# Two causal self attentions of a decoder's first layer: queries and keys stored as three bf16 parts, repeated by the loads

## The reference

```python
scores = (einsum('bhnd,bhmd->bhnm', q_r, k_r) + einsum('bhnd,bhmd->bhnm', q_i, k_i)) / sqrt(hd)
probs = softmax(where(causal, scores, -inf))          # 4 x 16 heads of 256 x 256
...
att = einsum('bhqd,bhkd->bhqk', q, k) * scale          # second attention, d = 8
y = einsum('bhqk,bhkd->bhqd', softmax(where(causal, att, -inf)), v)
```

## Time and profile before

| | before |
|---|---|
| median of three runs | 2439.69 us |
| the three runs | 2427.64, 2544.63, 2439.69 us |
| the profiled execution | 2427.71 us, of which 2425.9 us from the first to the last instruction |
| TensorE's mean granted clock | 0.854 of 2.4 GHz |
| busy shares | PE 78%, DVE 51%, ACT 39%, POOL 21% |
| `p0`: first store to first load of `a0` | 28.18 to 62.99 us |
| `a0`: first load to the end of the block | 62.99 to about 160 us |
| `p1`: first store to first store of `c0` | 189.00 to 223.65 us |
| `a1`: first load to the first load of `ac` | 313.19 to 408.17 us |

### The profile page before, as it was taken

How to read it: one execution, slowest core, us unless ns; L and a number is a source line. 1 busy time by engine, 2 the same in 40 slices (tenths; PEclk the granted TensorE clock), 3 DMA queues, 4 the chain that set the end, 5 groups by cost and what they waited for, 6 DMA issues and landing times. The chain is left out here.

```text
span 2425.9 us, 44544 instructions
## 1 busy us (share of the span) xinstructions
PE 1897.7 (78%) x16613; PEld 1031.0 (42%) x16613; DVE 1242.4 (51%) x2710; ACT 946.8 (39%) x1346; POOL 512.7 (21%) x360
## 2 busy tenths in 40 slices
PE   2764366888889826998899588439999999997497
PEld 1542243233233423664455356314444444554365
DVE  2663267888788233335843356344555555551322
ACT  1432143266566422221155135222555555453133
POOL 2112112000000000002644100002545444543100
PEclk7885578699799857998999789765999999998699
DMA  8416922132222021100000000011222112210010
GB/s 230 106 41 199 292 56 67 47 82 68 68 62 62 15 92 39 39 26 0 1 1 2 1 1 15 11 44 29 47 49 46 35 42 49 47 24 1 18 35 26
DMA packets 171185, 128.26 MB, mean 53 GB/s; under 512 B 22084, under 2 KB 156428, under 8 KB 170508
## 3 DMA queue, kind: packets, MB, share of 16 engines
q1 hardware_dynamic: 171020, 125.97, 19.5%
HBM read 64.41 MB, written 38.68 MB: 42 GB/s over the span
## 5 line engine op out<-in xcount | busy, mean ns | idle before, releaser
L1819 DVE TENSOR_REDUCE ta_mxp<-ps 128x1 f32<-128x401 f32 x512 | 267.1, 570 | 280.3 <-PE ps L1738 280.2
L805 DVE TENSOR_REDUCE ac_mxp<-ps 128x1 f32<-128x401 f32 x512 | 272.9, 567 | 48.2 <-PE ps L652 41.3
L1842 ACT ACTIVATE ta_prob<-ps 128x2048 f32<-128x2048 f32 (+1 forms) x112 | 196.6, 1755 | 148.2 <-PE ps L1774 148.2
L877 ACT ACTIVATE ac_prob<-ps 128x1024 f32<-128x1024 f32 (+1 forms) x208 | 210.3, 1024 | 105.6 <-PE ps L688 104.1
L652 PE MATMUL ps<-ac_kb,ac_qz 50*128 50x401 bf16 x512 | 180.9, 380 | 41.0 <-DVE ac_mxp L805 19.9
L1738 PE MATMUL ps<-ta_kb,ta_qb 96*128 96x401 bf16 x512 | 139.4, 357 | 16.2 <-DMA ta_kb<-ta_kh 12.2
L720 PE MATMUL ps<-ac_prob,ac_vs 128*32 128x256 f32 (+1 forms) x1664 | 146.6, 425 | 3.8 <-ACT ac_prob L877 3.7
L1770 PE MATMUL ps<-qxf,ta_k 32*128 32x256 f32 (+1 forms) x1664 | 134.7, 407 | 12.8 <-ACT ta_shiftT L1860 9.2
L652 PEld LDWEIGHTS ps<-ac_kb,ac_qz 50*128 50x128 bf16 x512 | 48.1, 95 | 202.7 <-DVE ac_mxp L805 172.1
L2283 PE MATMUL ps<-xT,e_wi 128*128 128x512 f32 x256 | 116.1, 608 | 15.4 <-DMA e_wd<-in_e_down 10.9
L688 PE MATMUL ps<-ac_qb,ac_kb 50*128 50x256 bf16 (+1 forms) x832 | 117.4, 291 | 4.8 <-issue 3.5
(11 more groups left out here) (322 smaller groups left out, 3600.0 us busy)
## 6 DMA issues: line engine op xcount, KB each, us to landing
ta_kb<-ta_kh SPq DMA_DIRECT2D x128, 100.1 KB, 2.2
vc<-c_vt SPq DMA_DIRECT2D x48, 256.0 KB
ac_vs<-vc SPq DMA_DIRECT2D x16, 768.0 KB
ac_kb<-kc SPq DMA_DIRECT2D x32, 200.1 KB, 3.3
ta_kb<-ta_kl SPq DMA_DIRECT2D x64, 100.1 KB, 2.2
v<-p_vt SPq DMA_DIRECT2D x16, 256.0 KB
a_vs<-v SPq DMA_DIRECT2D x32, 128.0 KB
e_wi<-in_e_in SPq DMA_DIRECT2D x8, 512.0 KB, 3.5
```

What stands on the lines that cost most here:

```text
L805: v.tensor_reduce(o, i, AX.X, ALU.max).then_inc(scores_read.s, 1)
L877: a.activation(prob[0:rows, ring, 0:n], banks[0:rows, 0:n], ACT.Exp, scale=scale).then_inc(exp_done.s, 1)
L1819: v.tensor_reduce(mxp[:, qt * G + g, c:c + 1], k.ps[:, turns.bank(slot), 0:401], AX.X, ALU.max).then_inc(scores_read.s, 1)
L1842: a.activation(prob[0:rows, n % 3, :, 0:w], k.ps[0:rows, 2:6, 0:w], ACT.Exp, scale=scale).then_inc(exp_done.s, 1)
```

## The change

Four of the kernel's scratches, `q0`, `k0`, `q1` and `k1`, are made with `thin=True`. The class had both ways in it already; nothing else differs. The scratches of the context attention (`qc`, `kc`) stay as they were.

```diff
-                q0, k0 = Scratch(nc, "q0", 16, N, "q"), Scratch(nc, "k0", 16, N, "k")
+                q0, k0 = (Scratch(nc, n + "0", 16, N, n, thin=True) for n in "qk")
...
-                q1, k1 = Scratch(nc, "q1", 8, N, "q"), Scratch(nc, "k1", 8, N, "k")
+                q1, k1 = (Scratch(nc, n + "1", 8, N, n, thin=True) for n in "qk")
```

## The result

The kernel became slower by about 1%: 2451.61 us (median of 14 runs, 2438.58 to 2461.41) against 2429.66 (14 runs of the kernel before, 2422.70 to 2439.69 but for one of 2544.63). The ratio, which leaves that one out, is 1.0092, with a 95% interval of 1.0074 to 1.0110. Forecast were 2466 us and a range of 2440 to 2503, most likely within 2%. The profiled execution of the kernel after took 2456.53 us, 2454.8 of them from the first to the last instruction.

What follows compares the result with a forecast made beforehand. The prediction took stores to be on the path in p0 and p1, and a0 bound by compute with loads hidden by 1.2 us. Its terms, -12.2 - 6.4 + 27 + 30 = +38, gave 2466 us, range 2440 to 2503.

Steps and rivals of the forecast that it cites:

- Stores of `p0`: Stage p0: sixteen thin stores replace the old transfers of queries and keys, values start at 41.5 instead of 53.70: -12.2 us.
- The landing of the first stores: In p0: unit 0's stores land 2.2 us after issue, so unit 4's first part can start at 31.5.
- the ring: In p0: units wait for earlier units' stores to land before reuse; one more landing would put the gain at 10.
- The price of a store: In p0: a thin store of 192 KB costs 0.81 us by bytes, 0.54 if the issue alone counted.
- the readiness of unit 7: In p0: unit 7 is complete at 40.4 and its stores issued at 41.5, when the values' stores start.
- Stores of `p1`: Stage p1: eight thin stores of queries and keys take 6.5 instead of 12.9 us: about -6.4, range 5 to 8.
- Loads of `a0`: Loop of a0: SP's thirteen issues a step, 0.49 per small load, make the period 6.5 us; with clock falls +27 us.
- a clock that stays down: Slower rival in a0 and a1: steps at 1.2 GHz, middle 7.6 us, become the period; total +56, 2484 us; chance 0.13.
- Loads of `a1`: Loop of a1: the same count of loads with half the bytes, priced as in a0: +30 us.
- the price of an issue: In a1: each 8 partition load holds SP for 0.49 us, taken from loads of 16 partitions.
- Dear 8 partition loads: Slower rival in a1: each load holds SP for 0.59 us, period 7.7; total +56, 2484 us; chance 0.27.
- Cheap issues: Faster rival in a0 and a1: issues cost 0.32 us in a row, period about 5.0; -17, 2411 us; chance 0.10.

Runs made afterwards that it cites:

- loads alone: Kernel before with stores and array unchanged, only the loads of queries and keys cut into six by slot: 2472.55 us, ratio 1.0161.
- early gate: Changed kernel with SP allowed to load queries and keys of step s + 3 some 4 us sooner: 2446.32 us, 1.0092 against the kernel before.
- ACT's help: Changed kernel with the six key loads of each step issued by ACT instead of SP: 2430.83 us, ratio 1.0011 against the kernel before.
- the second attention alone: Kernel before with only q1 and k1 made thin, q0 and k0 as before: 2434.72 us, ratio 1.0021.
- three stores: Changed kernel with each thin store made by three transfers of one part, 64 KB each: 2467.65 us, one execution.
- context late: Changed kernel with the 3.2 MB load of the context begun after a0 instead of ahead of p0: 2445.17 us, 1.0076 against the kernel before.
- the first attention alone: Kernel before with only q0 and k0 made thin, q1 and k1 as before: 2446.84 us, ratio 1.0055.

## Why the prediction was right, and where it was not

**The direction and the mechanism held.** The stores gain, the loads lose more, and the loss is SP's issue time. The loads alone, the kernel with the early gate and the one with ACT's help say so from three sides.

**Stores of `p0`, -9.3 for -12.2.** The landing of the first stores was off. The forecast set unit 4's first part at 31.5, with the 2.2 us of the earlier trace rows for the landing of unit 0's stores. DVE's timeline of after has it at 33.03, and unit 7 complete at 39.43 + 3.08 = 42.5 instead of 40.4:

```profile
33.03 0.43 DVE L453 CAST p_part<-p_full 128x512 bf16<-128x512 f32 x1 [4.00 <-DMA q<-p_part]
...
39.43 3.08 DVE L457 TENSOR_TENSOR p_part<-p_rest,p_part 128x512 bf16<-128x512 f32 x3
```

Unit 0's stores were issued at 27.16 and released it 5.9 us later, although their issues took a fraction of that. The median of a landing hid that the first one stands behind the context's load; with that load moved away unit 4 starts at 29.21. The values' stores then began at 43.78 instead of 41.5, which is 2.3 of the missing 2.9 us; they took 6.69 us instead of 6.09, which is the rest. The prediction named the ring as a limit and put its low end at 10; the measured gain lies just below it. The price of a store was off too, 0.81 by bytes where it held SP for 0.37 to 0.52, but that cost nothing: as the forecast itself has it, the readiness of unit 7 set the end.

**Stores of `p1`, -5.7 for -6.4.** Within its range of 5 to 8. Queries and keys take from 205.63 to 209.53 + 2.79 = 212.32, 6.7 us for the 6.5 that were taken. That the numbers meet is in part luck: 6.5 was eight stores by bytes, and eight stores at 0.43 in the median hold SP for about half of the 6.7 us, with pauses between them.

**Loads of `a0`, +26.0 for +27.** This step held with its working. Twelve issues take 112.08 - 106.35 = 5.73 us, 0.48 each, where 0.49 was forecast; the step takes 6.45 us and 6.7 in the mean, where 6.5 and, with the clock, 6.8 were forecast; step 13 starts (158.83 - 53.67) - (142.63 - 62.99) = 25.5 us later, forecast 23.9 + 3.3. PE's waits are shorter than thought, 14.6 / 9 = 1.6 us for 2.1, and the clock falls in some steps, as expected. PE's timeline of after, the first score matmul of two steps, and the stretches behind the second (columns as in the earlier trace rows):

```profile
93.69 0.23 PE L656 MATMUL ps<-a_kb,a_qb 96*128 96x128 bf16 x1 [1.47 <-DMA a_kb<-k]
...
100.11 0.28 PE L656 MATMUL ps<-a_kb,a_qb 96*128 96x128 bf16 x1 [1.70 <-DMA a_kb<-k]
```
```profile
93.70:95.20 1.50, 1.50 (x32) 1.26 (x32) 1.36 (x3) 0.37 (x1) 0.50 (x1) 1.00 0.47 133
...
100.10:101.80 1.70, 1.69 (x16) 1.62 (x16) 1.22 (x3) 0.00 (x0) 0.72 (x1) 0.50 0.30 84
101.80:103.50 1.70, 1.70 (x19) 0.76 (x18) 0.07 (x1) 1.35 (x3) 0.00 (x0) 0.53 0.26 75
103.50:105.20 1.70, 1.70 (x22) 1.28 (x22) 1.00 (x2) 0.41 (x1) 0.00 (x0) 1.00 0.24 65
```

After a wait of 1.47 us PE goes on at 2.4 GHz; after one of 1.70 it goes on at 1.2 GHz for some 3.4 us and is then back. The rival of a clock that stays down falls with the last row, and with the mean step of 6.7 us where it has 7.6.

**Loads of `a1`, +12.5 for +30.** This is the term that failed. It was 17.5 us too high; the stores' shortfall of 3.6 hid part of that, and 14 us remained in the total. The step that failed is the price of an issue: 0.49 was taken, "since the loads of 16 are nearest in shape", and the 8 partition loads held SP for 0.34 each at the start and for 4.75 us in twelve, 0.40 each, in the loop. The mean step shrank from the forecast 6.8 to 5.6 us, and step 13 started 413.70 - 324.06 = 89.6 us after the first load, where it had been 77.1: +12.5. Five kernels with this same `a1` (after, the second attention alone, loads alone, three stores, context late) show +8.8 to +13.3. The row of one 8 partition load in the earlier trace rows, at 0.33, had been the right witness; the prediction names it and takes the loads of 16 all the same. The direction stood without this term, on `a0`'s, but that the time came out within the range owes something to its width: 63 us had room for a term that was more than twice too large.

The Trainium skill, page "DMA: Bandwidth & Descriptors", section "Why a DMA increments its semaphore by 16 and not by 1", has the number of engines follow from what divides the slowest dimension of both sides, up to 16. The section says nothing of the price of an issue; that a transfer on fewer engines is dearer to issue was a reading that the forecast tried. The runs show the opposite for 8 and 4 adjacent partitions, 0.34 us against 0.45 for 16; and the loads to every sixth partition, still 16 of them, took 0.69, so that the count of engines doesn't order these prices.

**The rivals.** Dear 8 partition loads (0.59) fell with 0.34 to 0.40. The clock that stays down fell. Cheap issues fell in `a0`; in `a1` its price of 0.32 was nearly met at the start, but not its result: in the loop twelve loads, the address calculations and the values still need 5.45 us a step, more than PE's 4.9.

The Trainium skill, same page, section "Issuing engines are not separate DMA queues", says that issuing from several engines saves only the sequencer's time for the issues, usually small relative to the transfer. The first half agrees with the kernel in which ACT took three of SP's thirteen issues of a step: three at 0.48 are 1.4 us, and the step fell by 6.45 - 5.02 = 1.4 (the gate, which was opened earlier in it too, had by itself left the step at 6.45). The second half may hold for a single transfer: an issue of 0.48 us stands against a median of 1.8 us to its landing, for the loads of this size in the kernel with the first attention alone. It misleads where many stand on one queue: the issues of a step take 5.8 of its 6.45 us in `a0`, and they are its bound.

**Open.** Why 65 partitions and a spread destination are dear and 8 adjacent ones cheap is not shown; only the prices are. The early gate and ACT's share were not tried in one kernel with the context's load in its old place. Keys alone thin, into adjacent partitions, was not tried, nor another share for ACT than three or six slots.

## What to carry to other kernels

When a transfer is cut into many, count the issues on the queue that makes them and compare issues times price with the step they feed, before asking whether the transfer itself is hidden: here a queue that was idle for most of each 4.88 us step became the bound with thirteen issues in it. Take the price from a row of the same shape, even a single one, if it stands right behind another issue as these will, rather than from many rows of a shape that is merely near. And if the saving elsewhere is real, look for an engine with idle sequencer time to share the issues, and start its share early enough.

## What the runs showed of the hardware

- An issue on SP's queue costs by shape: in a row 0.45 us for 16 adjacent partitions (32 KB), 0.34 for 8 (16 KB) and also for 4 (8 KB), a little more with address calculations between; in the loops 0.69 for 16 partitions that lie six apart, and 0.81 for 8 such.
- A store of 128 partitions held SP for about the same time whatever its bytes: a median of 0.43 us at 64 KB, 0.49 at 128 KB on average, and 0.43 to 0.49 at 192 KB.
- The first unit's stores, issued behind a load of 3.2 MB, released their tile 5.9 us after the issue; with that load moved away it was 29.21 - 26.35 = 2.9.
- ACT issues the same loads at about the same price, 0.32 us for a single one and 1.75 / 4 = 0.44 in a row, between its activations.
- The length of `ac`, with the same code, differed by 21 us between profiled executions (440.9 to 462.1); the granted clock over the stage was 0.85 in the shortest and 0.81 in the longest, so the difference goes with its stretches of 1.2 GHz; what sets them off in one execution and not in another was not followed up.
